# Expert layers of a two-layer decoder: slots inverted on chip, tiles fetched by indirect gathers, the first layer's residual and norm in slot order

## The reference

```
x = x + mamba(layernorm(x));  x = x + cross_attention(layernorm(x), ctx)
x = x + experts0(layernorm(x))
x = x + shared_kv_attention(layernorm(x));  x = x + hard_cross(layernorm(x), ctx)
x = x + experts1(layernorm(x))

experts0(x): e = argmax(softmax(x @ w_router + b_router)), p = max(softmax(...))      # 8 experts
             p * (relu(x @ w1[e] + b1[e]) @ w2[e] + b2[e])                            # 256 -> 512 -> 256
experts1(x): e = argmax(softmax(x @ Wr.T))
             y = gelu(x @ W1[e] + b1[e]) @ Wo + bo + x                                # 256 -> 1024 -> 256
             (y - mean) * rsqrt(var + 1e-12) * gamma + beta
```

## Time and profile before

| | |
|---|---|
| device time, three executions | 1107.5, 1115.8, 1118.95 us; median 1115.8 |
| the profiled execution | 1117.67 us, its span 1115.5 us |
| PE busy, clock granted in the mean | 925.6 us (83%), 0.913 |
| DVE, ACT, POOL busy | 631.5, 464.0, 292.8 us |
| first expert stage, from its first DMA to the first transpose of the next stage | 402.0 to 533.4 us |
| second expert stage, to the end | 953.2 to 1115.5 us |

### The profile page before, as it was taken

How to read it: one execution, slowest core, us unless ns; L and a number is a source line. 1 busy time by engine, 2 the same in 40 slices (tenths; PEclk the granted TensorE clock), 3 DMA queues, 4 the chain that set the end, 5 groups by cost and what they waited for, 6 DMA issues and landing times. The chain is left out here.

```text
span 1115.5 us, 13009 instructions
## 1 busy us (share of the span) xinstructions
PE 925.6 (83%) x4004; PEld 468.0 (42%) x4009; DVE 631.5 (57%) x1319; ACT 464.0 (42%) x922; POOL 292.8 (26%) x288
## 2 busy tenths in 40 slices
PE   5878888999999858992799999979588897438975
PEld 2435534333332346661455555544222224313554
DVE  4856558888888241223365556535688883413534
ACT  3785345777777600220333333312047673112310
POOL 7125636000000002003165555522200000183014
PEclk9989999999999975996899999988769999568998
DMA  6040052033228041112810000003211100532000
GB/s 209 1 142 0 1 107 45 16 55 53 54 50 296 1 193 53 58 56 61 346 41 1 0 1 1 1 24 77 47 26 37 38 19 0 211 123 71 24 10 29
DMA packets 44520, 71.88 MB, mean 64 GB/s; under 512 B 10194, under 2 KB 31746, under 8 KB 43306
## 3 DMA queue, kind: packets, MB, share of 16 engines
q1 hardware_dynamic: 41322, 65.29, 20.0%
q0 software_dynamic: 2176, 5.38, 1.4%
q10 hardware_dynamic: 960, 0.43, 0.1%
HBM read 50.57 MB, written 11.01 MB: 55 GB/s over the span
## 5 line engine op out<-in xcount | busy, mean ns | idle before, releaser
L1064 DVE TENSOR_REDUCE c_amx<-PS 128x1 f32<-128x512 f32 x256 | 158.8, 683 | 29.3 <-PE PS L964 29.1
L1154 ACT ACTIVATE c_aE<-PS 128x512 f32<-128x512 f32 x256 | 132.6, 602 | 47.1 <-PE PS L976 46.9
L1836 POOL TENSOR_SCALAR s_Pn<-s_Pr,s_rs 128x512 f32<-128x512 f32 x64 | 100.1, 1566 | 101.6 <-DVE s_rs L1863 101.4
L964 PE MATMUL PS<-c_aKs,c_aQs 99*128 99x512 bf16 x256 | 95.4, 384 | 7.1 <-DMA c_aQs<-area 3.9
L976 PE MATMUL PS<-c_aQs,c_aKs 99*128 99x512 bf16 x256 | 94.5, 380 | 3.5 <-ACT c_aE L1154 2.3
L1064 DVE TENSOR_REDUCE h_amx<-PS 128x1 f32<-128x512 f32 x128 | 79.9, 684 | 25.5 <-PE PS L964 25.4
L68 POOL TENSOR_SCALAR rstd<-mv 128x4 f32<-128x4 f32 x10 | 2.3, 233 | 346.9 <-DVE mv L91 346.8
L1920 ACT ACTIVATE s_Pr<-PS,s_nmx 128x512 f32<-128x512 f32 x64 | 44.0, 688 | 116.2 <-DVE s_nmx L1856 116.2
L1854 DVE TENSOR_REDUCE s_mx<-PS 128x1 f32<-128x512 f32 x64 | 44.3, 691 | 69.1 <-PE PS L1967 69.1
L1154 ACT ACTIVATE h_aE<-PS 128x512 f32<-128x512 f32 x128 | 67.0, 602 | 32.4 <-PE PS L976 32.2
L964 PE MATMUL PS<-h_aKs,h_aQs 99*128 99x512 bf16 x128 | 55.3, 437 | 21.5 <-DMA h_aQs<-h_q_stack 20.7
(11 more groups left out here) (383 smaller groups left out, 1679.9 us busy)
## 6 DMA issues: line engine op xcount, KB each, us to landing
area<-in_e_w SPq DMA_DIRECT2D x16, 512.0 KB, 9.6
area<-in_g_w SPq DMA_DIRECT2D x8, 1024.0 KB, 16.5
c_aKs<-area SPq DMA_DIRECT2D x48, 128.0 KB
g_B<-in_g_b SPq DMA_DIRECT2D x1, 4096.0 KB, 11.8
c_aQs<-area SPq DMA_DIRECT2D x48, 64.0 KB
early<-in_ctxT SPq DMA_DIRECT2D x2, 1024.0 KB, 8.3
e_B<-in_e_b SPq DMA_DIRECT2D x1, 2048.0 KB, 7.3
ctx_T<-in_h_ctxT SPq DMA_DIRECT2D x1, 2048.0 KB, 13.8
```

The source lines that it names most:

```text
L964: pe.matmul(PS[:, n % MB, :], self.Qs[u % 3][:, j, qt * P:(qt + 1) * P], self.Ks[u % 3][:, j % self.KH, half * BANK:(half + 1) * BANK], st ...
L1064: dve.tensor_reduce(self.mx[:, qt, j, half:half + 1], PS[:, n % MB, :], AX.X, ALU.max).then_inc(self.max_done, 1)
L1154: act.activation(self.E[kt % 2][:, j, :], PS[:, MB + x % XB, :], ACT.Exp, scale=0.25).then_inc(self.exp_done, 1)
L1836: pool.tensor_scalar(Pn[g % NPB][:, :], Pr[g % NPB][:, :], rs[:, g % NPB:g % NPB + 1], None, ALU.mult).then_inc(pn_ready, 1)
```

## The change

**Inverse of the sort (both layers).** DVE no longer writes a row's slot for POOL to scatter by. The new class `SlotInverse` finds for each slot which row belongs there: DVE writes the slot of a row as tile and place (`tile1`, `r`), a one-hot matrix of the place (`R`) and the row's number times a one-hot of the tile (`V`); 8 small bf16 matmuls of the two sum up the number of the row in each slot, which DVE turns into indices `src`. The argmax by `max` and `max_index` becomes a maximum, a comparison and a second maximum.

**First layer.** `XN` and `X` are stored side by side as rows of 2 KB (`rows_in`) by plain DMAs, early in the stage. POOL gathers each of the 15 tiles from there by `src` into one of three `Xs` (`RING`). DVE multiplies by the probability (brought into slot order by 8 more small matmuls), adds the residual, takes statistics and normalises tile by tile, in slot order; POOL scatters each finished tile, x and its norm side by side, to `rows_out`; SP loads `XN` and `X` for the next stage from it, and the next stage starts from the loaded `XN` (its DVE does no norm). The loop in hardware is written out, the scatter, the loads, the store to `ys` and the 8 gathers go, and the `Context` matmuls stand behind the tiles.

**Second layer.** `XN` and `X` are stored early; POOL gathers each pair's tile itself, and the 8 sorted tiles of `XN` and `X` (`SR`, in the place of `X` and `XN`) between the pairs' gathers. The row numbers come from the inverse too (`ids`), so `XR`, its copies on ACT, its scatter and both loads back go. The zeroing of `Hall` now stands ahead of the gathers. The zeroing of `xs` in the first stage of the kernel (L3142) goes.

```diff
+class SlotInverse:
+    def vector(self, dve, c, slotf):
...
+        c.link(dve.tensor_tensor(self.ge[:, :, :], slotf[:, :].unsqueeze(2).to_broadcast(wide),
+                                 self.iotaP.unsqueeze(1).to_broadcast(wide), ALU.is_ge))
+        c.link(dve.tensor_reduce(self.tile1[:, :], self.ge[:, :, :], AX.X, ALU.add))
+        c.link(dve.scalar_tensor_tensor(out=self.r[:, :], in0=self.tile1[:, :], scalar=-float(P), in1=slotf[:, :],
+                                        op0=ALU.mult, op1=ALU.add))
+        for h in range(2):
+            i = slice(h * TB, (h + 1) * TB)
+            dve.tensor_tensor(self.R[:, i, :], self.iota_m.unsqueeze(1).to_broadcast([P, TB, P]),
+                              self.r[:, i].unsqueeze(2).to_broadcast([P, TB, P]),
+                              ALU.is_equal).then_inc(self.R_ready, 1)
+        c.link(dve.tensor_tensor(self.TH[:, :, :], self.tile1[:, :].unsqueeze(2).to_broadcast(wide),
+                                 self.iota.unsqueeze(1).to_broadcast(wide), ALU.is_equal))
+        dve.tensor_scalar(self.V[:, :, 0, :], self.TH[:, :, :], self.rowid, None, ALU.mult).then_inc(self.V_ready, 1)
+        dve.tensor_tensor(self.V[:, :, 1, :], self.TH[:, :, :], self.next_tile.unsqueeze(2).to_broadcast(wide),
+                          ALU.mult).then_inc(self.V_ready, 1)
+    def tensor(self, pe):
+        pe.wait_ge(self.V_ready, 2)
+        for i in range(NT):
+            pe.wait_ge(self.R_ready, i // TB + 1)
+            last = pe.matmul(self.bank[:, 0:2 * self.W], self.R[:, i, :], self.V[:, i, :, :].rearrange("p a w -> p (a w)"),
+                             start=(i == 0), stop=(i == NT - 1))
+        last.then_inc(self.mm, 1)
+    def vector_sources(self, dve, c):
+        dve.wait_ge(self.mm, 1)
...
+        dve.tensor_scalar(self.src[:, :], self.d[:, :], -float(P), 0.0, ALU.add, ALU.max).then_inc(self.src_ready, 1)
...
 # experts0_stage, SP
+            sp.dma_start(whole[:, :, rows_of(1)], X[:, :, :]).then_inc(rows_stored, 16)
+            for b in range(B):
+                i = slice(b * TB, (b + 1) * TB)
+                sp.wait_ge(nm.xn_ready, b + 1)
+                sp.dma_start(whole[:, i, rows_of(0)], XN[:, i, :]).then_inc(rows_stored, 16)
...
+            for n in range(RING):
+                used(sp, scattered, TILES - RING + n)
+            back = rows_out[0:T, :].rearrange("(t p) c -> p t c", p=P)
+            for b in range(B):
+                i = slice(b * TB, (b + 1) * TB)
+                sp.dma_start(XN[:, i, :], back[:, i, rows_of(0)]).then_inc(sh.xn_back[b], 16)
+            sp.dma_start(X[:, :, :], back[:, :, rows_of(1)]).then_inc(sh.x_back, 16)
+            sh.context.store(sp)
 # experts0_stage, POOL
+            def gather(t):
+                if t >= RING:
+                    pool.wait_ge(xsT_mm, t - RING + 1)
+                    pool.wait_ge(xb_ready, t - RING + 1)
+                pool.indirect_dma_start(out=Xs[t % RING][:, :], out_offset=None, in_=rows_in,
+                                        in_offset=bass.IndirectOffsetOnAxis(ap=inv.src[:, t:t + 1], axis=0),
+                                        ).then_inc(gathered[t % RING], 16)
...
+            for t in range(TILES):
+                if t + RING < TILES:
+                    gather(t + RING)
+                if t > 0:
+                    scatter(t - 1)
+                inverse_deviation(t)
+            scatter(TILES - 1)
 # experts0_stage, DVE, per tile: hidden(t + 1), normalise(t - 1), result(t)
+                dve.tensor_tensor(Hs[t % 2][:, :], PS[:, 1 + t % 2, :], B1[:, bass.ds(e * F, F)], ALU.add).then_inc(h_sum, 1)
+                dve.scalar_tensor_tensor(out=XB[t % 2][:, :], in0=B2[:, bass.ds(e * D, D)], scalar=prob_s[:, t:t + 1],
+                                         in1=Xs[t % RING][:, rows_of(1)], op0=ALU.mult, op1=ALU.add).then_inc(xb_ready, 1)
...
+                dve.scalar_tensor_tensor(out=z, in0=PS[:, 5 + t % 2, 0:D], scalar=prob_s[:, t:t + 1],
+                                         in1=XB[t % 2][:, :], op0=ALU.mult, op1=ALU.add).then_inc(z_ready, 1)
+                dve.bn_stats(st6[:, t, :], z).then_inc(st_ready, 1)
+                dve.bn_aggr(mv[:, t, :], st6[:, t, :]).then_inc(var_ready, 1)
+                dve.tensor_scalar(Zs[t % RING][:, rows_of(0)], Zs[t % RING][:, rows_of(1)], mv[:, t, 0:1],
+                                  rstd[:, t:t + 1], ALU.subtract, ALU.mult).then_inc(out_ready, 1)
 # experts1_stage, SP: X, XN in two halves to xn_rows, XN again beside X, then B1, B2, W2; no more loads
 # experts1_stage, POOL
+            for p in range(RING):
+                gather(p)
+            pool.wait_ge(nm.xT_done, KD * B)
+            pool.wait_ge(rows_stored, 32)
+            for p in range(RING, PAIRS):
+                gather(p)
+                if p - RING < NT:
+                    gather_rest(p - RING)
...
+                pool.tensor_tensor(SR[:, i, 0:D], SR[:, i, 0:D], B2[:, :], ALU.add)
+                last = pool.tensor_tensor(SR[:, i, D:2 * D], SR[:, i, D:2 * D], gb[:, 1, :], ALU.add)
 # experts1_stage, ACT
-            act.activation(XR[:, :, 0:D], X[:, :, :], ACT.Copy).then_inc(xr_ready, 1)
-            act.wait_ge(rows_in, 16)
-            act.activation(XR[:, :, D], rows_here[:, :], ACT.Copy).then_inc(xr_ready, 1)
             nm.scalar(act)
```

More of the change, by code:

```diff
@@ L2380, in _ @@
-            load(0, 0)
-            load(1, 1)
-            tiles_loop(sp, step)
-            if first:
-                sh.context.store(sp)
-            for p in range(2):
-                sp.wait_ge(stored[p], 16 * ((SLOT_TILES + 1 - p) // 2))
-            if not first:
-                for b in range(B):
-                    tiles = slice(b * TB, (b + 1) * TB)
-                    sp.wait_ge(out_ready, b + 1)
-                    sp.dma_start(sh.out[:, tiles, :], X[:, tiles, :]).then_inc(sh.out_stored, 16)
-                sp.wait_ge(sh.out_stored, 16 * B)
+            sp.dma_start(small[:, :], A["e_small"]).then_inc(small_in, 16)
@@ L2426, in _ @@
+            for t in range(RING):
+                gather(t)
+            for t in range(TILES):
[5 more added lines that the diff above has]
+            scatter(TILES - 1)
         @block.vector
@@ L2613, in _ @@
-            if not first:
-                pe.wait_ge(w2_in, 16)
-            def transpose_x(t, p):
-                pe.wait_ge(xs_in[p], (t - p) * 8 + 16)
-                if not known_below(t, 1):
+            pe.wait_ge(ones_set, 2)
+            pe.wait_ge(trib_made, 1)
+            hot = OHb[:, :, :].rearrange("p i e -> p (i e)")
+            pe.matmul(PS[:, 5, 0:NT * EXP], trib[:, :], hot, start=True, stop=False, skip_group_check=True)
+            for i in range(1, NT):
+                pe.matmul(PS[:, 5, i * EXP:NT * EXP], ones[:, :], hot[:, 0:(NT - i) * EXP], start=False,
+                          stop=(i == NT - 1), skip_group_check=True)
@@ new lines, in _, with spread_probabilities @@
+            for i in range(NT):
+                last = pe.matmul(PS[:, 6, 0:EXP], ones[:, :], OHb[:, i, :], start=(i == 0), stop=(i == NT - 1))
+            last.then_inc(rank_mm, 1)
+            inv.tensor(pe)
+            def spread_probabilities():
+                pe.wait_ge(vp_ready, 3)
+                for i in range(NT):
+                    last = pe.matmul(PS[:, 7, 0:3 * inv.W], inv.R[:, i, :], VP[:, i, :, :].rearrange("p n w -> p (n w)"),
+                                     start=(i == 0), stop=(i == NT - 1))
+                last.then_inc(prob_mm, 1)
@@ L2626, in up @@
                 pe.wait_ge(xsT_ready, t + 1)
-                if not known_below(t, 2):
+                if t >= 2:
                     pe.wait_ge(h_sum, t - 1)
-                for half in range(NB1):
-                    for k in range(KD):
-                        last = pe.matmul(PS[:, 1 + p * NB1 + half, :], XsT[p][:, k, :],
-                                         W1[:, k, bass.ds(e * F + half * BANK, BANK)],
-                                         start=(k == 0), stop=(k == KD - 1))
@@ L2634, in up @@
[L2634 to L2642 removed]
+                for k in range(KD):
+                    last = pe.matmul(PS[:, 1 + t % 2, :], XsT[t % 2][:, k, :], W1[:, k, bass.ds(e * F, F)],
+                                     start=(k == 0), stop=(k == KD - 1))
```

684 lines of the change are left out of this document (317 added, 367 removed).

## The result

The changed kernel takes 1082.8 us (median of four executions, 1078.4 to 1086.4) where the kernel before takes 1114.9 (four, 1107.5 to 1119.0): a ratio of 0.972 with a 95% interval of 0.965 to 0.979. Timed again on another chip, six executions against eleven, it was 1083.75 against 1118.6: 0.969 (0.966 to 0.972). It is faster by about 3%, some 32 to 35 us, where 45.6 were forecast.

A forecast was written before the change was run, and what follows sets the result against it. PE was taken as the bound within the tiles and pairs, its waits around them as the gain: -21.7 (stage one) - 24.9 (stage two) + 1 = -45.6 us off the median 1115.8, 1070 us; forecast 1066 to 1075, range 1061 to 1084.

The forecast's parts named there:

- rival 1: Both expert loops: POOL's indirect DMAs become the bound, up to 28 us lost, 1075 to 1098 us; chance 0.16.
- rival 5: End of stage one: the barrier or a load keeps the 24.06 us of idle PE, 1081 us; chance 0.05.
- Stage one up to the first tile: First expert stage: first gather lands at 425.1, where the first tile's transpose stands at 434.87 now, -9.7 us.
- path two decides: Stage one's end: Context matmuls (8.8 us), copy and store end at 508.7, later than the last tile's scatter and loads, 506.1.
- The bound of -23.9: Stage one in all if every Context matmul is fast, so that the last tile's scatter and loads decide: -23.9 us.
- without these the router starts about 959.1: Second expert stage: without the wait for `XR` and the row numbers, the router starts about 959.1 instead of 961.13.
- May run partly at clock 1.00, in 4.6: Second stage's router: 4.6 instead of 6.96 us; logits -4.3 us with the earlier start, bounds -2.0 and -4.4.
- The rule against it: A DVE instruction with two SBUF inputs blocks GpSimd reading SBUF: scatters beside such additions may take up to one addition longer.
- hidden by 0.6, charged 1: Second stage: the 16 additions ready at 1031.4, DVE wants them at 1032.0; 1 us charged in case they are slower.
- Rival 3: Stage two's first pairs wait: gather shares DMA engines with 8.4 MB or `W2` lands late; 1073 to 1078 us; chance 0.14.
- Rivals 1, 2, 5: The 2 here: POOL's indirect DMAs 2.63 us or more apart take the whole gain, 1132 us at 3.0; chance 0.03.
- Rival 4: Context matmuls don't delay the barrier and some waits inside the tiles go: 1062 to 1067 us; chance 0.12.

The follow-up runs named there:

- the first experiment: Changed kernel with GpSimd's eight memsets of `Hall` in the second expert stage waiting for both halves of the norm: 1081.6 us, ratio 0.9665 to the kernel before.

## Why the prediction came out as it did

The direction and the range held (1082.8 within 1061 to 1084); the point, 1070, was 13 us too low. That the range held is luck in part: its upper half was there for POOL as the bound (rival 1) and for stage one's end staying as it was (rival 5), and neither came; the largest part of what did come, the memsets beside the norm, was in no rival. By its own steps:

- **Stage one up to the first tile, -9.7**: -7.3 in the first profile (23.3 us after the norm's start where before has 32.9, -9.6, in the second). The difference is the router: 6.97 us at clock 0.50 throughout against 4.90 at 0.73 in the mean; before had 4.6. From the logits to the first transposes it is 12.7 us in both, and 12.5 were counted: `src` comes 0.5 sooner, the gather lands 3.6 us after issue instead of 2.8.
- **The tiles, "1 us off for the waits"**: 1.6 and 1.8 us in the two profiles.
- **After the last tile**: 11.7 us from the last tile to the next transposes where 13.1 were counted. The Context matmuls took 9.3 and 9.7 instead of 8.8; from their end (508.11) to the next transposes 2.55 us pass where 4.3 were taken for copy, store and barrier. The choice of "path two decides" was right by about 2 us only. The bound of -23.9 for fast matmuls should read -24.3 by its own terms.
- **Stage one in all, -21.7**: -21.2 and -23.4. Behind it PE lost 0.8 to 1.6 us on `s_wv`, which the sum had at nothing.
- **Stage two, "without these the router starts about 959.1"**: this is the step that failed. It costed what the change takes away ahead of the router and left out what it moves there: the memsets of `Hall`, until then behind the scatters, now beside the norm. +5.4 us at the router's start; shown by the first experiment, in which the logits came as forecast.
- **"May run partly at clock 1.00, in 4.6"**: it ran 6.97 us at 0.50, +2.4. Its bounds named that case. In the five runs with the memsets moved it took 4.6 to 5.1 us in three and 6.97 in two; in the six with the norm stretched it took 6.97 each time.
- **From the logits to `src` and the first gather's landing**: held, 14.1 us from the logits to the first pair's matmuls where 14.3 were counted.
- **The first pair's 5.1**: 6.3 us to the next transpose, +1.2. **Pairs at 3.73 without a stop**: held, 3.7 each. **POOL hidden**: held.
- **The rule against it**: seen, and hidden. Five gathers issued while DVE adds into `Hall` from two operands in SBUF (L2913) last 1.64 us instead of 0.95: the one at 985.30 ends 0.82 us after the addition at 984.85 does. The gather of each pair, issued beside the addition that reads PSUM (L2905), keeps its 0.95. Two a pair leave POOL 0.8 us free, so PE doesn't see it.
- **The additions "hidden by 0.6, charged 1"**: 0.5 by their wait, and 1.7 more by the clock of one down projection (5.38 instead of 3.69), which two profiles with the same additions didn't show; what sets the clock there stays open.
- **Rival 3, the first pairs wait for the traffic**: not seen in the changed kernel, since its sources came so late that most of the 8.4 MB was through. It appeared when the memsets were moved: 3.5 us. The forecast's 1 us of slack was itself too good: `W2` was to land 24 us after the stage's start and landed 28.2 after it there, 29.7 in the changed kernel.
- **Rivals 1, 2, 5** fell: POOL left 0.8 us of each pair free, and the idle time at stage one's end went. The measured time lies in rival 1's span (1075 to 1098), but not for its reason. **Rival 4** came in small part: the Context matmuls set the barrier back by about 2 us, and the tiles gave 0.6 to 0.8 more than counted.

Together 5.4 + 2.4 + 1.2 + 0.5 + 1.7, less the 1 charged, are 10.2, which is what is missing (23.9 - 13.7). Of these only the 5.4 and the 0.5 are shown by an experiment to come from the change; the 2.4, the 1.2 and the 1.7 went with the granted clock, which differed between profiles of the same code. The stretches that the change doesn't touch gave 3.0 of the 37.2 us in the first profile and lost 1.7 in the second, whose span is 33.8 under before's; that is most of what lies between 37.2 and the 32 to 35 by medians.

## What to carry to other kernels

List what a change moves, not only what it adds: GpSimd's memsets cost nothing while VectorE waits and 5.4 us beside its norm. A gain on the way to a transfer uncovers the transfer's queue, so let loads and stores that are needed late be issued behind the first gather. Work put into a wait at a stage's end (Context, 9.3 us of it for about 2) is nearly free, the same work in front of a chain (12.5 us) is not.

## What the runs showed of the hardware

- Eight GpSimd memsets of 128x1024 f32 and eight VectorE `tensor_scalar` of 128x256 f32, side by side: 1093 against 972 ns for a memset (947 to 952 in the run with the memsets moved, one of them 1031), 1112 against 408 ns for a `tensor_scalar`, and 1.03 us from one pair to the next. In the run with the additions ahead of the gathers, 1.3 us of GpSimd's 128x256 additions lay beside VectorE's first small operations; one of these, a comparison of 64 columns, took 0.86 us instead of 0.22 and ended as the additions did.
- A gather of 128 rows of 1 KB lands, from issue to use, 3.0 us after issue with free queues, 5.5 to 6.5 with several MB of plain loads and stores issued before it still moving; of 2 KB rows 3.6 in nine profiles, 4.2 and 5.3 in the two with filled waits (in the twelfth TensorE came later).
- GpSimd's issue of a gather, of 1 or 2 KB rows, lasts 0.95 us while VectorE is idle, and as long beside an addition of VectorE that reads PSUM. Begun during one with two operands in SBUF (128x1024 f32, 1.28 us) it ends 0.82 us after that: 1.64 us long in the changed kernel (five times), up to 1.95 in the run with three gathers a pair. One begun within 0.05 us of the addition's start kept its 0.95. The first gather after the indices, beside several small operations, took 1.11 to 1.23.
- The router, the same 32 records, took 4.04 to 6.97 us from one profile to the next, at a mean granted clock of 0.90 to 0.50.
